# Masked cross-attention: keys of a head pair as one 128-row transfer, scores as two 64-row products a head

## The reference, cut to what matters

```python
def _L1_xattn_ref(q, k, v, mask, Wq, Wk, Wv, Wo):
    HEADS = 16
    B, Sq, Hd = q.shape            # 4, 128, 512
    H = HEADS
    d = Hd // H                    # 32
    scale = 1.0 / np.sqrt(d).astype(np.float32)
    qh = (q @ Wq.T).reshape(B, Sq, H, d).transpose(0, 2, 1, 3)
    kh = (k @ Wk.T).reshape(B, -1, H, d).transpose(0, 2, 1, 3)
    vh = (v @ Wv.T).reshape(B, -1, H, d).transpose(0, 2, 1, 3)
    scores = jnp.einsum('bhqd,bhkd->bhqk', qh, kh)
    scores = jnp.where(mask[:, None, :, :], jnp.float32(-1000000000.0), scores) * scale
    attn = jax.nn.softmax(scores, axis=-1)
    out = jnp.einsum('bhqk,bhkd->bhqd', attn, vh)
    out = out.transpose(0, 2, 1, 3).reshape(B, Sq, Hd)
    return out @ Wo.T

x = x + _L1_xattn_ref(_layernorm(x, axis=-1), ctx_1024, ctx_1024, mask_BxSxS2_bk1, ...)
```

## Time and profile before

| what | value |
|---|---|
| median of 3 runs | 2057.87 us |
| the profiled execution's own time | 2066.56 us |
| its span | 2064.8 us |
| granted TensorE clock, mean | 0.944 |
| masked cross-attention, main loop with prologue | about 735 to 1410 us |
| PE busy | 1857.7 us, 90% |
| VectorE, ScalarE, GpSimd busy | 1175.7, 974.7, 407.5 us |
| DMA | 293.51 MB, mean 142 GB/s |

### The profile page before, as it was taken

The page is one execution under the profiler, slowest core; times in us unless marked ns, Lnnn a source line. Parts: engine busy times, 40 slices in busy tenths (PEclk is TensorE's granted clock), DMA queues, the critical chain, the costliest instruction groups (busy, mean ns, idle before and its releaser), DMA issues. The chain is left out here.

```text
span 2064.8 us, 26143 instructions
## 1 busy us (share of the span) xinstructions
PE 1857.7 (90%) x9584; PEld 1503.8 (73%) x9584; DVE 1175.7 (57%) x2376; ACT 974.7 (47%) x2027; POOL 407.5 (20%) x300
## 2 busy tenths in 40 slices
PE   5998999988899989998999898797888779899997
PEld 4677878776787779996899697574545568778786
DVE  7666666654634356675677478593344355655544
ACT  4554545442343245664566367482223354554543
POOL 0433545450000042121113022220100011111110
PEclk9999999999999999998999899798999789999999
DMA  6122212106501697784677469571000445564520
GB/s 233 61 82 82 95 69 102 63 31 250 184 1 62 205 289 238 231 251 147 208 241 235 132 205 250 141 211 46 0 1 0 158 169 169 191 207 168 184 72 22
DMA packets 121597, 293.51 MB, mean 142 GB/s; under 512 B 10672, under 2 KB 83888, under 8 KB 107056
## 3 DMA queue, kind: packets, MB, share of 16 engines
q1 hardware_dynamic: 121456, 291.67, 43.9%
HBM read 221.38 MB, written 70.25 MB: 141 GB/s over the span
## 5 line engine op out<-in xcount | busy, mean ns | idle before, releaser
L1063 DVE TENSOR_TENSOR PTL<-bank,PTH 128x512 fp32r<-128x512 f32 x256 | 175.7, 686 | 119.9 <-ACT PTH L1061 118.2
L1061 ACT CAST PTH<-bank 128x512 fp32r<-128x512 f32 x256 | 149.9, 586 | 143.0 <-PE bank L1056 142.9
L1040 ACT ACTIVATE TT<-TT,MX 128x512 f32<-128x512 f32 x256 | 186.8, 730 | 11.0 <-DVE MX L1030 11.0
L1576 DVE TENSOR_TENSOR WS<-EW,WS 128x1024 fp32r<-128x1024 f32 (+1 forms) x120 | 141.1, 1180 | 75.7 <-ACT WS L1573 74.6
L1012 DVE CUSTOM_DVE_ANT_0 TT<-bank,MASK 128x512 f32<-128x512 f32 x256 | 174.0, 680 | 9.1 <-POOL KST L986 7.0
L1056 PE MATMUL bank<-IDN,TT 128*128 128x128 f32 x1024 | 161.9, 282 | 8.6 <-DVE PTL L1063 4.6
L1573 ACT CAST WS<-EW 128x1024 fp32r<-128x1024 f32 (+1 forms) x144 | 139.0, 976 | 58.4 <-PE bank L1593 54.7
L986 POOL CAST KST<-KST 32x1024 fp32r<-32x1024 f32 x86 | 87.8, 1046 | 339.6 <-DMA KST<-tmp_kh 332.3
L1077 PE MATMUL bank<-PTH,VG 128*128 128x256 f32 x512 | 142.1, 298 | 12.8 <-DMA VG<-tmp_v 12.6
L95 PE MATMUL bank<-BCH,WKT 128*128 128x256 f32 x512 | 149.4, 292 | 4.3 <-DVE BCL L579 2.3
L97 PE MATMUL bank<-BCH,WKT 128*128 128x256 f32 x512 | 146.8, 287 | 0.0
(11 more groups left out here) (310 smaller groups left out, 4679.9 us busy)
## 6 DMA issues: line engine op xcount, KB each, us to landing
EW<-in_ewg SPq DMA_DIRECT2D x48, 1024.0 KB, 4.7
tmp_v<-EV SPq DMA_DIRECT2D x32, 1024.0 KB, 4.9
VG<-tmp_v SPq DMA_DIRECT2D x32, 1024.0 KB, 5.9
EW<-in_ewg SPq DMA_DIRECT2D x24, 768.0 KB, 4.2
CT<-in_ctxT SPq DMA_DIRECT2D x32, 512.0 KB, 4.4
CN<-in_ctxN SPq DMA_DIRECT2D x32, 512.0 KB, 3.5
BCT<-in_ctxT SPq DMA_DIRECT2D x32, 512.0 KB, 3.4
tmp_kh<-EKH SPq DMA_DIRECT2D x64, 256.0 KB, 3.1
```

The lines of the kernel that those rows point to most:

```text
L1040: t_e[(n, kc)] = tick("act", act.activation(TT[:, sl, cs], TT[:, sl, cs], ACT.Exp, bias=MX[:, n % 4, 5:6], scale=SC1, accum_out=SUM[:, b % ...
L1061: t = tick("act", act.copy(PTH[:, q], bank[bk][:]))
L1063: t = free[bk] = tick("dve", dve.tensor_tensor(PTL[:, q], bank[bk][:], f(PTH[:, q]), ALU.subtract))
L1576: t_lo = tick(low, E[low].tensor_tensor(WS[:, s, 1, 0:n * w], src, f(WS[:, s, 0, 0:n * w]), ALU.subtract))
```

## The change

Keys are kept in DRAM as `[batch, feature, half, key]`, so that the 32 features of a head with both halves are 64 neighbouring rows, high and low interleaved, and a pair of heads is 128 rows. One DMA (two for the third slot) loads a pair; GpSimd's copy is gone; three slots now hold three pairs. The queries are written twice: `tmp_q1` has every high row twice, `tmp_q2` every low row twice. The score of a head is then two 64-row products, q1 by keys and q2 by keys, into one bank (start on the first, stop on the second), which adds the term low by low. `score_pair` issues for the two heads of a pair: first product of head 0 (rows 0 to 63), first of head 1 (rows 64 to 127), second of head 0, second of head 1, in every other step. The chunk order becomes head 0 and head 1 in turn, `score_max` handles one chunk a step, and `exp_chunk` runs four steps later than before relative to the scores.

```diff
-                    for dst, src in ((KDH, EKH), (KDL, EKL)):
-                        t = dma("sp", f"kw{e}", dst[b, rows, cols].rearrange("(a p) t -> p a t", a=2),
+                    for x, src in enumerate((EKH, EKL)):
+                        t = dma("sp", f"kw{e}", KD[b, rows, x, cols].rearrange("(a p) t -> p a t", a=2),
...
-        for src, dst in ((QH, D["qh"]), (QL, D["ql"])):
-            t_qd = dma("sp", "qd", dst.rearrange("(c p) t -> p c t", p=128), f(src[:]))
+        for src, dst in ((QH, D["q1"]), (QL, D["q2"])):
+            for x in range(2):
+                t_qd = dma("sp", "qd", dst.rearrange("(c p x) t -> x p c t", p=128, x=2)[x], f(src[:]))
...
-            dma("sp", f"ldqs{half}", f(QS[0:32, hs]), q_dram("qh", b)[:, hs])
-            dma("sp", f"ldqs{half}", f(QS[32:64, hs]), q_dram("qh", b)[:, hs])
-            t_qs[(b, half)] = dma("sp", f"ldqs{half}", f(QS[64:96, hs]), q_dram("ql", b)[:, hs])
+            for part, k in enumerate(("q1", "q2")):
+                rows = D[k].rearrange("(g p) t -> p g t", p=128)
+                t_qs[(b, half)] = dma("sp", f"ldqs{half}", f(QS[:, 4 * half:4 * half + 4, part]),
+                                      rows[:, 4 * half:4 * half + 4, 128 * b:128 * b + 128])
...
-            for dst, cs in halves:
-                t_hi = dma("sp", f"ldkh{sl}", f(dst[0:32]), KDH[b, rows, cs])
-            for dst, cs in halves:
-                t_lo = dma("sp", f"ldkl{sl}", f(dst[32:64]), KDL[b, rows, cs])
-            need("pool", t_hi, k_free[sl], ("pool", P.count["pool"]))
-            t_kl[n] = [[tick("pool", pool.tensor_copy(dst[64:96], f(dst[0:32]))), t_lo] for dst in KEYS[sl]]
+            rows = KD[b].rearrange("(g d) x t -> g (d x) t", g=8)[p % 8]
+            halves = [(KST[:, sl], slice(0, 2048))] if sl < 2 else [(KSA[:], slice(0, 1024)), (KSB[:], slice(1024, 2048))]
+            t_kl[p] = []
+            for j, (dst, cs) in enumerate(halves):
+                t_kl[p].append(dma("sp", f"ldk{sl}{j}", f(dst), rows[:, cs]))
...
+        def score_pair(i):
+            p, kc = i // 4, i % 4
+            b, half, ks = p // 8, p % 8 // 4, p % NK
+            need("pe", t_kl[p][-1 if kc > 1 else 0], t_qs[(b, half)])
+            bks = []
+            for h in range(2):
+                bks.append((0, 1, 4)[sb_n % 3])
+                sb_n += 1
+                need("pe", free[bks[h]])
...
+            for part in range(2):
+                for h in range(2):
+                    r = slice(64 * h, 64 * h + 64)
+                    m = pe.matmul(bank[bks[h]][:], QS[r, p % 8, part, :], keys[r, cs], start=(part == 0),
+                                  stop=(part == 1))
+                    if part:
+                        t_s[(2 * p + h, kc)] = (bks[h], tick("pe", m))
+            if kc == 3:
+                k_free[ks] = t_s[(2 * p + 1, 3)][1]
+                load_keys(p + NK)
...
-                score_chunk(g + 12)
-                exp_chunk(g + 8)
+                if g % 2 == 0:
+                    score_pair(g // 2 + 6)
+                score_max(g + 12)
+                exp_chunk(g + 4)
```

More of the change, by code:

```diff
@@ L876, in build @@
         A = Region(B1.at)
-        QS = A("QS", [128, 16, 128], F32R)
+        QS = A("QS", [128, 8, 2, 128], F32R)
         NK = 3
@@ L965, in load_vg, with load_keys @@
                               VD[b, h // 2].rearrange("p (k d) -> p k d", k=16))
-        def load_head(n):
-            if n >= 64:
+        def load_keys(p):
+            if p >= 32:
                 return
-            b, h = n // 16, n % 16
-            if h == 0:
+            b, sl = p // 8, p % NK
+            if p % 8 == 0:
                 while kv_done[b] is None:
@@ L995, in build @@
         t_e, t_m = {}, {}
-        def score_chunk(g):
+        t_s = {}
+        def score_pair(i):
             nonlocal sb_n
-            n, kc = g // 4, g % 4
+            p, kc = i // 4, i % 4
+            if p >= 32:
+                return
+            b, half, ks = p // 8, p % 8 // 4, p % NK
[5 more added lines that the diff above has]
+                need("pe", free[bks[h]])
+            keys = KEYS[ks][kc // 2]
+            cs = slice(512 * (kc % 2), 512 * (kc % 2) + 512)
+            for part in range(2):
[8 more added lines that the diff above has]
+                load_keys(p + NK)
+                if p % 4 == 3:
+                    qs_free[half] = k_free[ks]
+                    if b < 3:
+                        load_qs(b + 1, half)
@@ L1001, in score_chunk, with score_max @@
+        def score_max(g):
+            p, kc, h = g // 8, g % 8 // 2, g % 2
+            n = 2 * p + h
             if n >= 64:
                 return
[L1003 to L1009, removed]
@@ L1010, in score_chunk @@
-            t = tick("pe", pe.matmul(bank[bk][:], QS[0:96, h, :], keys, start=True, stop=True))
-            need("dve", t)
+            b, sl = p // 8, n % 4
+            bk, t = t_s[(n, kc)]
+            need("dve", t_mk[b], tt_free[sl][kc], t)
             t2 = free[bk] = tick("dve", dve.tensor_tensor_reduce(
                 TT[:, sl, 512 * kc:512 * kc + 512], bank[bk][:], MASK[:, b % 2, 512 * kc:512 * kc + 512],
-                1.0, NEG, ALU.add, ALU.max, MX[:, n % 4, kc:kc + 1]))
+                1.0, NEG, ALU.add, ALU.max, MX[:, sl, kc:kc + 1]))
@@ L1015, in score_chunk @@
             if kc < 3:
                 return
[L1017 to L1023, removed]
+            if n % 16 == 15:
                 mask_free[b % 2] = t2
@@ L1027, in score_chunk @@
             need("dve", t2)
-            t = tick("dve", dve.tensor_reduce(MX[:, n % 4, 4:5], MX[:, n % 4, 0:4], AX.X, ALU.max))
+            t = tick("dve", dve.tensor_reduce(MX[:, sl, 4:5], MX[:, sl, 0:4], AX.X, ALU.max))
             need("dve", t)
-            t = tick("dve", dve.tensor_scalar(MX[:, n % 4, 5:6], MX[:, n % 4, 4:5], -SC1, None, ALU.mult))
-            t_m[n] = t
+            t_m[n] = tick("dve", dve.tensor_scalar(MX[:, sl, 5:6], MX[:, sl, 4:5], -SC1, None, ALU.mult))
         def exp_chunk(g):
-            n, kc = g // 4, g % 4
+            p, kc, h = g // 8, g % 8 // 2, g % 2
+            n = 2 * p + h
             if n >= 64:
                 return
-            b, h, sl, cs = n // 16, n % 16, n % 4, slice(512 * kc, 512 * kc + 512)
+            b, sl, cs = p // 8, n % 4, slice(512 * kc, 512 * kc + 512)
             need("act", t_m[n])
-            t_e[(n, kc)] = tick("act", act.activation(TT[:, sl, cs], TT[:, sl, cs], ACT.Exp, bias=MX[:, n % 4, 5:6],
-                                                      scale=SC1, accum_out=SUM[:, b % 2, h, kc:kc + 1]))
+            t_e[(n, kc)] = tick("act", act.activation(TT[:, sl, cs], TT[:, sl, cs], ACT.Exp, bias=MX[:, sl, 5:6],
+                                                      scale=SC1, accum_out=SUM[:, b % 2, n % 16, kc:kc + 1]))
         t_ots = [None]
@@ L1162, in build @@
         for n in range(NK):
-            load_head(n)
+            load_keys(n)
         load_qs(0, 1)
@@ L1168, in build @@
         for g in range(12):
-            score_chunk(g)
-            if g >= 4:
-                exp_chunk(g - 4)
+            if g % 2 == 0:
+                score_pair(g // 2)
+            score_max(g)
+            if g >= 8:
+                exp_chunk(g - 8)
             if g in (4, 8):
@@ L2090, in program @@
     D = {k: nc.dram_tensor("tmp_" + k, s, F32, kind="Internal").ap()
-         for k, s in (("kh", [4, 512, 2048]), ("kl", [4, 512, 2048]), ("v", [4, 8, 128, 2048]),
-                      ("qh", [512, 512]), ("ql", [512, 512]))}
+         for k, s in (("k", [4, 512, 2, 2048]), ("v", [4, 8, 128, 2048]),
+                      ("q1", [1024, 512]), ("q2", [1024, 512]))}
     build(nc, I, out, D, stop)
```

11 lines of the change are left out of this document (2 added, 9 removed).

## The result

After the change the kernel takes 2086.59 us (median of 4 runs, 2086.21 to 2086.87), before 2057.24 us (4 runs, 2054.77 to 2063.93): the ratio is 1.0137, with an interval of 1.0113 to 1.0161, so 29.35 us slower. The forecast was 2099 us, within 2060 to 2126. The profiled execution after took 2086.42 us (span 2085.0) and that of before 2066.56 (9 us above its median), so the two traces differ by only 19.9 us.

What follows compares the result with a forecast made beforehand. PE was taken as the bound while background runs; afterwards PE, VectorE and ScalarE are close. Terms 34.8 + 3 + 5 - 1.5 + 1 = 42.3 us, less 1 for hidden drains, on 2057.87 gave 2099 us, range 2060 to 2126.

Steps and rivals of the forecast that it cites:

- rival 1: Changes of row configuration around the scores: only one way drains PE, 0.20 us a pair; 2080 us, chance 0.14.
- Surroundings of the scores, with background: Masked cross-attention, PE full: draining into and out of 64-row products costs 0.40 us a pair, 87 pairs, 34.8 us.
- Columns: Score products: four 64-row products run as two side-by-side couples, 0.46 us as before, so nothing gained or lost.
- Without background: Masked cross-attention after background pieces run out: PE's average step becomes 1.37 us; +3 us for 80 steps (-6 to +12).
- Writes of the queries: Doubled query writes ahead of the next context load on the SP queue: +5 us (0 to 7).
- First scores: PE's first wait for keys: no GpSimd copy, but a larger first key DMA; -1.5 us (-5 to +3).
- Loads of V: PE's waits of 12.6 us for V, with a 1 MB key load ahead: 0 us (-5 to +6).
- Slack of the exponentials: Slack between maxima and exponential grows from one step to two, removing ScalarE's 11.0 us of waits; counted as nothing.
- no drain: Second rival: changing row configuration around the scores costs PE nothing; +4.5 us, 2062 us, chance 0.10.
- faster: Third rival: without a drain, relief without background, in the first wait and in V's loads; -17 us, 2041 us, chance 0.07.
- no side by side: Fourth rival: the four score products run serially, +0.46 us a pair with background; 2156 us, chance 0.05.
- dearer: Fifth rival: changes of row configuration around the scores cost 0.60 us a pair; +65 us, 2123 us, chance 0.14.

Runs made afterwards that it cites:

- the version without the change of configuration: Kernel after the change, with one 128-row product for each chunk's score instead of two of 64 rows, mixing both heads: 2049.33 us, 0.9943 of before.
- the experiment on one half: Kernel after the change, with all four score products of a pair on rows 0 to 63, head 1's scores left out: 2142.46 us, 1.04 of before.
- the last experiment: Kernel before, exponentials later, mask early, keys interleaved, a second read of high rows replacing GpSimd's copy, 96-row product kept: 2070.3 us, 1.0061 of before.

## Why the prediction was right, and where it was off

The mechanism held, and the time is 12 us below the forecast. The time alone would decide little: the range from 2060 to 2126 holds rivals 1, 2 and 5 as well, and rival 1's 2080 is nearer to 2086.59 than 2099 is. What decides is the trace and the experiments. By its own terms:

- **Surroundings of the scores, with background: 34.8 us.** Held. 0.38 us a pair in one place, 0.39 over 64 pairs, 0.41 against the version without the change of configuration. The split of 0.20 in and 0.20 out was nearly so (0.17 and 0.21). The second couple starts 0.31 instead of 0.23 us after the first, but that is no cost of its own: with a single couple the way out is as long (0.12 + 0.10).
- **Columns: 0.** Held; a couple costs 0.22 to 0.24 us. The reason I had for it was right in part only: that the products alternate is not what makes them overlap.
- **Without background: +3 us.** From close 3 to close 4, 32 of these pairs, after loses 106.2 - 104.6 = 1.6 us, and 20 pairs in its middle take 2.81 us each before and after. Right within its bounds.
- **Writes of the queries: +5.** Held: the stall grew by 4.95 us, and without the doubled write the time fell by 5.8.
- **First scores: -1.5.** Measured -3.6, for the right reason.
- **Loads of V: 0 (-5 to +6).** This is the term that was mis-sized: the 12.6 us of waits all went, beyond its lower bound. I counted bytes ("the DMA load in the loop is the same"), and in bytes it is; but where no background runs the engines were full at 238 GB/s before and move 330 at 0.87 after, and a key load is asked for earlier. This is most of the distance between +41 and the result. Its size is one trace's: with the same loads of V other traces have 8.2 to 17.2.
- **Slack of the exponentials: nothing.** Held: ScalarE's 11.0 us of waits are gone, and giving the slack alone to before moved the time by no more than its interval.

With the measured terms the sum is 87 x 0.38 + 1.6 + 5 - 3.6 - 12.6 = 23.5 us, where the traces show 25.2 at the next stage. The medians say 29.35. The other 4 us are within what before's runs leave open: its median is 2057.24 in the 4 runs of the result, and 2062.22, 2062.15 and 2058.31 in the 15, 7 and 25 runs made along with the experiments; and the waits for V change by as much between traces.

The rivals: "one way drains" (2080) falls by the weight loads, which idle both ways; "no drain" and "faster" fall by the experiment without the change of configuration, which is what they would have looked like (2049); "no side by side" by the experiment on one half; "dearer" by 0.38 to 0.41.

## What to carry to other kernels

On a full PE, price a form of matmul by its neighbours as well as its columns: two 64-row products side by side cost one, but putting them between 128-row ones cost 0.4 us each time, so count the changes, not only the products (two products between the changes instead of four left that cost at 0.39; longer groups were not tried). Price a transfer by the rows that it fills and by the outer dimension of its source, and read the DMA share beside the GB/s: a full share at few GB/s points to the shape of the transfers, not to much data. Before removing a helper engine's work (here 128 copies), look whether anything but one first wait hangs on it.

## What the runs showed that I had not expected

- The order in which products on the two halves of the rows are issued makes no difference (2085.43 against 2086.59 us).
- With key transfers whose source has an outermost dimension of 2, long stretches ran at 33 to 66 GB/s and the kernel was 322 us slower, though the number of key transfers was halved.
- Waits for V of 12.6 us went away with either of two changes, and came back only where both were absent (before, and 13.8 us in the last experiment). The queries' transfers changed shape too in after, so their share in this stays open.
- A transfer's landing time says how full the queue is before it says anything of its shape: 4.4 and 13.8 us for the same 256 KB into 32 rows.
